# Reordering the tail of a sequence's fourth tile in a two-layer attention and feed-forward kernel (one core)

## The chip, the cores and the metric

The kernel runs on one core of one Trainium2 chip. The metric is the device time of one execution in microseconds, the median of three runs for the kernel before.

## The reference

An input of 8 x 512 x 256 passes a depth-2 transformer, a test-time-training layer, and the same transformer again. Each transformer layer does, with everything in float32:

```python
h = shift_token(x)                       # second half of the channels comes from the row above
q, k, v = jnp.split(h @ wqkv, 3, axis=-1)
q = l2norm(q) * qs;  k = l2norm(k) * ksc
q, k = rotary_xpos(q, k)
o = local_attention(q, k, v)             # windows of 128, each looks at itself and the one before
x = x + o @ wo
h = shift_token(x)
mu = h.mean(-1, keepdims=True);  var = h.var(-1, keepdims=True)
h = (h - mu) / jnp.sqrt(var + 1e-05) * lg + lb
a, g = jnp.split(h @ w1 + b1, 2, axis=-1)
x = x + (a * jax.nn.gelu(g, approximate=False)) @ w2 + b2
```

## The kernel before, in words

There are 4 layers (two before the middle stage, two behind it), and each is run over 8 sequences of 512 rows: 32 sequences in all. A sequence is cut into four tiles of 128 rows, t = 0 to 3. A product is made of three matmuls on split operands (a high and a low part of each side), which stand on lines 1213 to 1215 (`split_product`), so h2T, oT, hT and uT each have a high part, written by ScalarE, and a low part, written by VectorE or GpSimd as the rest.

Each engine has its own instruction list, written out by hand in a function `sequence` of that engine, and semaphores tie the lists together. Every list is worked off strictly in order; a wait holds what stands behind it.

In a tile, TensorE does the scores (`S`, line 1285), the output projection of the tile before (`WO`), q, k and v of the tile ahead (`A1`), transposes of the probabilities (`PT` and `PTE`, lines 1305 and 1312), the value product (`PV`, line 1336) and transposes of the rotated q and k of the tile ahead (`A2`, line 1258). Where it would have to wait, `fill` puts matmuls of the second feed-forward product of the previous sequence (`W2`, line 1471): 16 units for a tile, which the table `cuts` shares out.

Behind the fourth tile comes the feed-forward part. It has two halves of 256 rows each. For each half the normalized rows h2 are made on VectorE (`LN_moments`, `LN_apply`, line 1995) with a power on GpSimd (`LN`, line 708), are transposed on TensorE (`H2T`: line 1375 for the row above the first, line 1377, line 1381), copied out as h2T (ScalarE lines 957 and 959, VectorE lines 1950 and 1951), and multiplied with W1 in six jobs (`W1`): job 0 is the narrow one (6 matmuls), jobs 1 to 5 have 12 each, job 6 to 11 are those of the second half.

Half 0 needs tiles 0 and 1 and the boundary row, so its inputs are there early. Half 1 needs tile 3: behind the last WO, VectorE adds it to Y (`WO`, line 1944), takes the statistics of the half rows (`halves`, lines 1963 and 1964), SyncE's queue moves them by a row with three small transfers (`move_stats`, lines 420, 405 and 423), and then come moments (lines 1979, 1977, 1983), power and apply of the last three columns. TensorE's list has the transposes of half 1 behind job 4 of half 0:

```python
for mt in range(MT):
    W1(L, b, 0, mt, bool(nxt))
    ...
    if mt == 4:
        H2T(L, b, 1)
```

The attention output of the fourth tile is summed in o_sum (`O_first` on ScalarE, `O_add` on VectorE, line 1931), its high part is copied by ScalarE (line 931) and its low part made by VectorE (`O`, line 1937).

Of the kernel before, what the change touches and what calls it, by code (L numbers as in the profile page):

```python
# [39 lines left out]
P = 128  # L40
# [19 lines left out]
E_BANK = 3  # L60
O_BANK = (6, 4)
REST = HID - (MT - 1) * P
# [9 lines left out]
def build(nc, A):  # L72
    ctx = ExitStack()
    with ctx:
# [571 lines left out]
        def _(e):  # L646
# [72 lines left out]

            def sequence(L, b, prev, nxt):  # L720
                for t in range(NT):
# [116 lines left out]
        def _(e):  # L838
# [114 lines left out]
            def H2T(L, b, half):  # L953
# [5 lines left out]
                e.activation(columns(h2T, 0, lo, 2 * P), cut(bank[4][:, :], KT), ACT.Copy).then_inc(h2t_hi, 1)  # L959
# [5 lines left out]
            def G(L, b, half, i):  # L965
# [6 lines left out]
                if mt < MT - 1:  # L972
                    e.activation(gg[:, job % 2, :], bank[job % 4][:, 256:512], ACT.Gelu,  # L973
                                 bias=b1[:, L % 2, 1, mt:mt + 1]).then_inc(gelu_done, 1)
                else:
                    e.activation(gg[0:REST, job % 2, :], bank[job % 4][64:64 + REST, 0:256], ACT.Gelu,
# [17 lines left out]
            def sequence(L, b, prev, nxt):  # L994
                for t in range(NT):
# [20 lines left out]
                    if t == 3:  # L1016
                        O(L, b, t)
# [8 lines left out]
                    if t == 3:  # L1026
                        H2T(L, b, 0)
# [182 lines left out]
        def _(e):  # L1210
# [50 lines left out]
            def S(L, b, t, half, more):  # L1261
# [6 lines left out]
                for j in banks:  # L1268
                    if j == 2 and (t < NT - 1 or more):
                        e.wait_ge(ht_lo, at(ht_lo, n + 2))  # L1270
                    if t == 0:
                        e.wait_ge(u_done, at(u_done, 12 * b + (96 * L + j - 3)))
# [94 lines left out]
            def H2T(L, b, half):  # L1367

                done = 9 * b + (72 * L + 4 * half)
                if half == 0:  # L1370
                    e.wait_ge(pt_sb, at(pt_sb, 3 * idx(L, b, 3) + 3))
                    e.wait_ge(o_added, at(o_added, sums(L, b, 3) + 2))
# [5 lines left out]
                for k in range(KT):  # L1378
                    for i in range(2):
                        e.wait_ge(h2n_done, at(h2n_done, done + half + 2 * k + i + 1))  # L1380
                        mm = e.transpose(bank[4][:, (2 * k + i) * P:(2 * k + i + 1) * P],  # L1381
# [3 lines left out]
            def W1(L, b, half, i, more):  # L1385
# [9 lines left out]
                if job < 4:  # L1395
                    e.wait_ge(nb_done, at(nb_done, 4 * n + 4))
                    if more:
                        if job == 0:
                            e.wait_ge(kt_sb, at(kt_sb, n + 2))
                        if job == 1:  # L1400
                            e.wait_ge(qt_sb, at(qt_sb, q_steps(n + 2)))
                        if job == 2:
                            e.wait_ge(ht_lo, at(ht_lo, n + 3))
                else:
                    e.wait_ge(u_done, at(u_done, 12 * b + (96 * L + job - 3)))
                if job == 6:
                    out = bank[job % 4][:, 0:256]
# [8 lines left out]
                for g in range(0 if job == 6 else 2 if mt < MT - 1 else 1):  # L1416
                    for k in range(KT):
                        mm = split_product(bank[job % 4][:, g * 256:(g + 1) * 256],
# [56 lines left out]
            def sequence(L, b, prev, nxt):  # L1475
                for t in range(NT):
                    ahead = (L, b, t + 1) if t < NT - 1 else nxt and (*nxt, 0)
                    ahead2 = (L, b, t + 2) if t < NT - 2 else nxt and (*nxt, t - 2)
                    cuts = ((5, 6, 11, 13, UNITS), (0, 0, 7, UNITS), (0, 0, 7, UNITS), (0, 0, 7, UNITS))[t]
# [30 lines left out]
                    else:  # L1510
                        PV_first(L, b, t)
                    if ahead and t:
# [59 lines left out]
            def mid_zT(p, i, *ks):  # L1572
                e.wait_ge(t_h[i], at(t_h[i], p + 1))
                for k in ks:
# [4 lines left out]
                    else:  # L1579
                        e.wait_ge(u_done, at(u_done, 12 * (B - 1) + 96 * (DEPTH - 1) + 8 + k + 1))  # L1580
# [262 lines left out]
        def _(e):  # L1843
# [5 lines left out]
            def rotary(L, b, t, i, terms=(0, 1)):  # L1849
# [18 lines left out]
                if t == 1:  # L1868
# [77 lines left out]
            def H2T(L, b, half):  # L1946
# [4 lines left out]
                e.tensor_tensor(columns(h2T, 1, lo, 2 * P), cut(bank[4][:, :], KT), columns(h2T, 0, lo, 2 * P), ALU.subtract).then_inc(h2t_lo, 1)  # L1951
# [50 lines left out]
            def U(L, b, half, i):  # L2002
# [10 lines left out]
                e.scalar_tensor_tensor(ut[0:rows, job % 2, :], bank[job % 4][0:rows, 0:256], b1[0:rows, L % 2, 0, mt:mt + 1],  # L2013
# [89 lines left out]
            def sequence(L, b, prev, nxt):  # L2103
                for t in range(NT):
# [28 lines left out]
                    else:  # L2133
                        for j in range(1, 4):
                            if L == 0 and b == 0 and t == 1 and j == 2:
                                entry_apply(0, 3)
                            R(L, b, t, j)
                            if ahead and j == 2:
                                rotary(*ahead, 0)
                        if ahead:  # L2140
                            rotated(*ahead, 0)
                            squares(idx(*ahead), 0)
                        WO(L, b, t - 1)
                        if t == 3:
                            LN_moments(L, b, 0)
                            halves(L, b, t - 1)
                        if ahead:
# [3 lines left out]
                        if L == 0 and b == 0 and t == 3:  # L2151
                            beta()
                        if t < 3:
# [356 lines left out]
```

## Time and profile before

| | |
|---|---|
| median of 3 runs | 2497.58 us (2497.53 to 2497.6) |
| the profiled execution | 2497.31 us |
| its span | 2495.5 us |
| TensorE busy | 2448.4 us, 98% of the span |
| VectorE, ScalarE, GpSimd busy | 79%, 73%, 63% |
| granted TensorE clock | 0.999 |

The profile is one execution. A row of the timeline gives start, length, engine, line, operation and operands; like instructions behind one another are merged (x8), and in brackets stands how long the engine was idle ahead of it and who released it. Matmuls overlap: a matmul's row is 0.28 us long where the next one starts 0.12 us later. So TensorE's start times tell more than its busy time, and a wait under about 0.17 us shows as no idle time at all.

### The profile page before, as it was taken

Reading aid. Unit: us, or ns where it says so; the run is one execution under the profiler, and the core shown is the slowest. Engines: PE = TensorE matmul, PEld = TensorE weight load, DVE = VectorE, ACT = ScalarE, POOL = GpSimd, SP = SyncE. Lnnn points to the kernel's source line nnn. Section 1 sums busy time; section 2 is a strip of 40 time slices with the busy share of each in tenths; the row PEclk is TensorE's granted clock in tenths of the full one; section 3 lists DMA queues with packets and bytes.
Section 4 is the critical chain, followed back from the end, with each engine's and each line's share of the span. In section 5 each row is a group of like instructions: output and inputs, shape, how many; then the busy total and the mean of one; then the engine's idle time right before and its main releaser. Section 6 shows DMA issues by size and latency. Waiting matters only on the chain. (4 is left out here: it accounts for less than half of the span.)

```text
span 2495.5 us, 80211 instructions
## 1 busy us (share of the span) xinstructions
PE 2448.4 (98%) x29515; PEld 2190.9 (88%) x29515; DVE 1981.1 (79%) x6502; ACT 1809.9 (73%) x5232; POOL 1562.9 (63%) x1798
## 2 busy tenths in 40 slices
PE   8999999999999999999999999999999999999999
PEld 7889989999999889998766898999999988999998
DVE  7888888887877887777656888777777788888886
ACT  6778777777777777776554787777777777777776
POOL 6666667666666666665212676666666667666665
PEclk9999999999999999999999999999999999999999
DMA  3122011013000000005101000000003100000000
GB/s 128 38 88 74 26 58 55 28 37 111 17 4 4 3 3 29 4 15 204 36 19 36 4 3 3 4 4 4 4 4 126 37 3 20 20 20 21 21 21 29
DMA packets 80115, 85.04 MB, mean 34 GB/s; under 512 B 38938, under 2 KB 66030, under 8 KB 78574
## 3 DMA queue, kind: packets, MB, share of 16 engines
q1 hardware_dynamic: 78430, 78.45, 9.7%
q8 instruction: 237, 3.88, 0.6%
q10 hardware_dynamic: 1296, 1.46, 0.2%
q14 instruction: 152, 1.25, 0.2%
HBM read 49.53 MB, written 26.74 MB: 31 GB/s over the span
## 5 line engine op out<-in xcount | busy, mean ns | idle before, releaser
L676 POOL TENSOR_TENSOR pr<-pr,rden 128x384 f32<-128x384 f32 (+1 forms) x480 | 410.1, 871 | 273.0 <-DVE rden L1918 268.1
L888 ACT ACTIVATE pr<-pr,nb 128x192 f32<-128x192 f32 (+1 forms) x1024 | 438.0, 430 | 170.5 <-DVE nb L1909 170.5
L1213 PE MATMUL bank<-h2T,w 128*128 128x256 f32 x1344 | 386.0, 287 | 3.2 <-issue 0.9
L1214 PE MATMUL bank<-h2T,w 128*128 128x256 f32 x1344 | 376.9, 280 | 0.0
L1215 PE MATMUL bank<-h2T,w 128*128 128x256 f32 x1344 | 376.8, 280 | 0.0
L1909 DVE CUSTOM_DVE_ANT_0 pr<-bank,maskb,r 128x192 f32<-128x192 f32 (+1 forms) x1024 | 347.4, 393 | 24.9 <-PE bank L1285 23.3
L718 POOL TENSOR_TENSOR uTl<-t,uTh 128x256 fp32r<-128x256 f32 x288 | 218.0, 762 | 181.0 <-ACT uTh L988 147.9
L1213 PE MATMUL bank<-wqkv,hT 128*128 128x512 f32 x768 | 304.9, 397 | 1.8 <-DVE nb L1909 1.5
L1214 PE MATMUL bank<-wqkv,hT 128*128 128x512 f32 x768 | 302.5, 394 | 0.0
L1215 PE MATMUL bank<-wqkv,hT 128*128 128x512 f32 x768 | 300.1, 391 | 0.0
L2013 DVE SCALAR_TENSOR_TENSOR t<-bank,b,t 128x256 f32<-128x256 f32 (+1 forms) x384 | 184.4, 481 | 109.2 <-POOL uTl L718 47.4
L1213 PEld LDWEIGHTS bank<-h2T,w 128*128 128x128 f32 x1344 | 254.0, 189 | 8.4 <-issue 6.2
L1214 PEld LDWEIGHTS bank<-h2T,w 128*128 128x128 f32 x1344 | 256.5, 191 | 0.0
L1215 PEld LDWEIGHTS bank<-h2T,w 128*128 128x128 f32 x1344 | 252.9, 188 | 0.0
L1471 PE MATMUL bank<-w2h,uTh 128*128 128x256 f32 x768 | 224.8, 294 | 0.0
L671 POOL TENSOR_TENSOR r<-ssg,small 128x8 f32<-128x8 f32 x128 | 214.9, 1679 | 10.7
L708 POOL TENSOR_TENSOR rs<-vare,small 128x4 f32<-128x4 f32 (+2 forms) x96 | 95.3, 993 | 200.0 <-DVE vare L1983 199.8
L660 POOL TENSOR_TENSOR r<-ssg,small 128x8 f32<-128x8 f32 x128 | 213.5, 1668 | 8.0
L1285 PE MATMUL bank<-kT,qT 64*64 64x64 f32 (+2 forms) x6656 | 205.9, 263 | 6.3 <-ACT kT L867 3.1
L973 ACT ACTIVATE t<-bank,b 128x256 f32<-128x256 f32 x320 | 150.8, 471 | 80.7 <-PE bank L1215 77.5
L1285 PEld LDWEIGHTS bank<-kT,qT 64*64 64x64 f32 x6656 | 183.8, 132 | 26.0 <-issue 8.4
L988 ACT ACTIVATE uTh<-t 128x256 fp32r<-128x256 f32 (+1 forms) x352 | 145.3, 413 | 80.9 <-DVE t L2013 78.0
(256 smaller groups left out, 7150.9 us busy)
## 6 DMA issues: line engine op xcount, KB each, us to landing
wqkv<-wqkv_split SPq DMA_DIRECT2D x18, 512.0 KB, 6.4
w<-w_split SPq DMA_DIRECT2D x3, 2816.0 KB, 10.8
Y<-in_x SPq DMA_DIRECT2D x8, 512.0 KB, 7.7
stt<-stt SPq DMA_DIRECT2D x256, 3.0 KB
out<-Y SPq DMA_DIRECT2D x8, 512.0 KB, 3.8
h<-out SPq DMA_DIRECT2D x7, 512.0 KB, 3.9
out<-h SPq DMA_DIRECT2D x7, 512.0 KB, 3.0
stt<-stt SPq DMA_DIRECT2D x192, 0.0 KB
```

What stands on the lines that cost most here:

```text
L660: e.tensor_tensor(r[:, t, 0, :], ssg[:, 0, :], minus_half, ALU.pow).then_inc(rk_done, 1)
L671: e.tensor_tensor(r[:, t, 1, :], ssg[:, 1, :], minus_half, ALU.pow).then_inc(rq_done, 1)
L676: e.tensor_tensor(probs(j, t), probs(j, t), rden[:, 2 * j:2 * j + 2].unsqueeze(2).to_broadcast([P, 2, w]), ALU.mult).then_inc(pn_done, 1 i ...
L718: e.tensor_tensor(uTl[:, half, JOBS[i], :], ut[:, job % 2, :], uTh[:, half, JOBS[i], :], ALU.subtract).then_inc(u_lo, 1)
L888: last = e.activation(probs(j, t)[:, g, :], probs(j, t)[:, g, :], ACT.Exp, bias=nb[:, hd:hd + 1], scale=-1.0, accum_out=den[:, hd:hd + 1])
L1213: e.matmul(out, left[0], right[0], start=first, stop=False)
L1214: e.matmul(out, left[0], right[1], start=False, stop=False)
L1215: return e.matmul(out, left[1], right[0], start=False, stop=last)
L1285: m = e.matmul(out[:, to:to + w, :], qT[rows, 0, p, HB * a:HB * a + HB], kT[rows, p, block:block + w, :], start=True, stop=True, skip_grou ...
L1471: mm = e.matmul(bank[bk][:, 0:D], left, right, start=(unit == 0), stop=(unit == UNITS - 1))
L1909: m = e.tensor_tensor_reduce(probs(j, t)[:, g, :], bank[j][:, g * 256:g * 256 + w], far, r[:, t, 1, place(hd):place(hd) + 1], FAR, ALU.add ...
L2013: e.scalar_tensor_tensor(ut[0:rows, job % 2, :], bank[job % 4][0:rows, 0:256], b1[0:rows, L % 2, 0, mt:mt + 1], gg[0:rows, job % 2, :], AL ...
```

## The change

It reorders the end of the fourth tile (t = 3). On TensorE the transposes of half 0's h2 move from behind the last W2 units to directly behind the value product, and job 0 of W1 moves ahead of the fourth tile's WO. Two W2 units move from behind A2 to ahead of the value product (`cuts`: 9 in place of 7). On VectorE the moments of half 0 move up between two reciprocals, the apply moves ahead of the last step of q's rotation, and a few small steps trade places; the low part of the attention output moves from VectorE to GpSimd (`O_lower`). On GpSimd the power moves ahead of the guard and power of k. On ScalarE the copy of h2T's first half moves ahead of the copy of the attention output. Half 0's transposes go to bank 3, and the W1 jobs take banks 2, 1, 0, 3 in place of 0, 1, 2, 3.

```diff
+H2T_BANK = (3, 4)
+JOB_BANK = (2, 1, 0, 3)
...
+            def O_lower(L, b, t):
+
+                n = idx(L, b, t)
+                for i in pair:
+                    e.wait_ge(o_hi, at(o_hi, 2 * n + i + 1))
+                    e.tensor_tensor(oT[:, 1, 2 * i:2 * i + 2, :].rearrange("p a c -> p (a c)"), o_sum[:, 2 * P * i:2 * P * i + 2 * P],
+                                    oT[:, 0, 2 * i:2 * i + 2, :].rearrange("p a c -> p (a c)"), ALU.subtract).then_inc(o_lo, 1)
...
+                    if t == 3:
+                        LN(L, b, 0)
                     if ahead and t:
                         guard_k(*ahead)
                     if ahead:
                         A1_k(*ahead)
                     if t == 3:
-                        LN(L, b, 0)
+                        O_lower(L, b, t)
...
                     if t == 3:
+                        H2T(L, b, 0)
                         O(L, b, t)
...
-                    if t == 3:
-                        H2T(L, b, 0)
...
-                    e.wait_ge(o_added, at(o_added, sums(L, b, 3) + 2))
...
-                    cuts = ((5, 6, 11, 13, UNITS), (0, 0, 7, UNITS), (0, 0, 7, UNITS), (0, 0, 7, UNITS))[t]
+                    cuts = ((5, 6, 11, 13, UNITS), (0, 0, 7, UNITS), (0, 0, 7, UNITS), (0, 0, 9, UNITS))[t]
...
+                    if t == 3:
+                        H2T(L, b, 0)
+                        fill(2)
...
-                    if t:
+                    if t in (1, 2):
                         fill(2)
-                    if t == 3:
-                        H2T(L, b, 0)
-                        WO(L, b, t)
                 for mt in range(MT):
                     W1(L, b, 0, mt, bool(nxt))
+                    if mt == 0:
+                        WO(L, b, 3)
...
+                            if t == 3 and j == 1:
+                                LN_moments(L, b, 0)
...
+                            LN_apply(L, b, 0)
+                            if ahead:
+                                rotated(*ahead, 1)
...
-                        LN_apply(L, b, 0)
-                        O(L, b, t)
+                        H2T(L, b, 0)
                         if prev:
                             W2(*prev, t)
-                        H2T(L, b, 0)
+                        if ahead:
+                            squares(idx(*ahead), 1)
```

Three places show it. TensorE behind the value product (pT, v) of the fourth tile, second sequence of the first layer. Before, the eight transposes of q and k follow, then W2 units:

```order
L1336 MATMUL bank<-pT,v 64x128 x16
L1336 MATMUL bank<-pT,v 64x64 x16
L1258 MATMUL bank<-ident,t 128x128 x8
L1471 MATMUL bank<-w2l,uTh 128x256
L1471 MATMUL bank<-w2h,uTl 128x256
```

Now (in the changed kernel's line numbers) the h2 transposes come first and then the W2 units:

```order
L1347 MATMUL bank<-pT,v 64x128 x16
L1347 MATMUL bank<-pT,v 64x64 x16
L1385 MATMUL bank<-lead,pick 128x2
L1391 MATMUL bank<-ident,h 128x128 x4
L1481 MATMUL bank<-w2h,uTh 128x256
L1481 MATMUL bank<-w2l,uTh 128x256
```

So the h2 transposes no longer stand behind the q and k transposes and nine W2 units. A little later on TensorE, before, all twelve matmuls of WO (wo, oT) stand ahead of W1 (h2T, w):

```order
L1213 MATMUL bank<-wo,oT 128x256
L1214 MATMUL bank<-wo,oT 128x256
L1215 MATMUL bank<-wo,oT 128x256
L1213 MATMUL bank<-h2T,w 128x256
L1214 MATMUL bank<-h2T,w 128x256
L1215 MATMUL bank<-h2T,w 128x256
```

Now six matmuls of W1's job 0 follow the q and k transposes, and WO begins behind them:

```order
L1269 MATMUL bank<-ident,t 128x128 x8
L1224 MATMUL bank<-h2T,w 128x256
L1225 MATMUL bank<-h2T,w 128x256
L1226 MATMUL bank<-h2T,w 128x256
L1224 MATMUL bank<-h2T,w 128x256
L1225 MATMUL bank<-h2T,w 128x256
L1226 MATMUL bank<-h2T,w 128x256
L1224 MATMUL bank<-wo,oT 128x256
L1225 MATMUL bank<-wo,oT 128x256
```

WO has six matmuls of W1 ahead of it that stood behind it. VectorE in the same tile, before, from the sums of q's squares to h2T's low part (h is h2, t are the rotation's buffers):

```order
L1896 TENSOR_REDUCE ssq<-sq 128x8
L1871 TENSOR_TENSOR t<-bank,rot 128x512
L1875 TENSOR_TENSOR t<-bank,rot 128x512
L1882 TENSOR_TENSOR t<-t 128x512
L1847 TENSOR_TENSOR hT<-bank,hT 128x2x128
L1931 TENSOR_TENSOR qT<-bank,qT 128x256 x2
L1991 TENSOR_TENSOR lead<-mv,rs 128x2
L1995 TENSOR_SCALAR h<-Y,mv,rs 128x128 x4
L1937 TENSOR_TENSOR oT<-qT,oT 128x256 x2
L2029 TENSOR_TENSOR Y<-bank,xb 128x256
L1950 TENSOR_TENSOR h2T<-bank,h2T 128x1
L1951 TENSOR_TENSOR h2T<-bank,h2T 128x2x256
```

Now:

```order
L1908 TENSOR_REDUCE ssk<-sq 128x8
L1883 TENSOR_TENSOR t<-bank,rot 128x512
L1887 TENSOR_TENSOR t<-bank,rot 128x512
L2003 TENSOR_TENSOR lead<-mv,rs 128x2
L2007 TENSOR_SCALAR h<-Y,mv,rs 128x128 x4
L1894 TENSOR_TENSOR t<-t 128x512
L1859 TENSOR_TENSOR hT<-bank,hT 128x2x128
L1943 TENSOR_TENSOR qT<-bank,qT 128x256 x2
L1962 TENSOR_TENSOR h2T<-bank,h2T 128x1
L1963 TENSOR_TENSOR h2T<-bank,h2T 128x2x256
L2041 TENSOR_TENSOR Y<-bank,xb 128x256
L1908 TENSOR_REDUCE ssq<-sq 128x8
```

The four h2 instructions stand three places earlier, the low part of oT is gone from this list, and the sum of q's squares stands at its end.

## Rows read from the trace of the kernel before

**Rows 1.** The page: busy time and share of each engine.

```profile
PE 2448.4 (98%) x29515; PEld 2190.9 (88%) x29515; DVE 1981.1 (79%) x6502; ACT 1809.9 (73%) x5232; POOL 1562.9 (63%) x1798
```

**Rows 2.** Waits of TensorE: total us, times, longest.

```profile
PE bank L1258 <- DVE t L1882: 9.4, 26, 0.4
```

**Rows 3.** Timeline of TensorE, fourth tile of one sequence: start, length.

```profile
1831.07 1.57 PE L1336 MATMUL bank<-pT,v 64*64 64x128 f32 x64
1833.00 1.09 PE L1258 MATMUL bank<-ident,t 128*128 128x128 f32 x8 [0.36 <-DVE t L1882]
1833.85 0.36 PE L1471 MATMUL bank<-w2l,uTh 128*128 128x256 f32 x1
...
1834.98 0.28 PE L1375 MATMUL bank<-lead,pick 128*128 128x2 f32 x2
...
1835.57 0.35 PE L1213 MATMUL bank<-wo,oT 128*128 128x256 f32 x1
...
1836.94 0.28 PE L1215 MATMUL bank<-wo,oT 128*128 128x256 f32 x1
1837.35 0.36 PE L1213 MATMUL bank<-h2T,w 128*128 128x256 f32 x1
1837.55 0.28 PE L1214 MATMUL bank<-h2T,w 128*128 128x256 f32 x1
```

**Rows 4.** Timeline of TensorE, third tile of the same sequence.

```profile
1817.77 1.57 PE L1336 MATMUL bank<-pT,v 64*64 64x128 f32 x64
1819.27 1.09 PE L1258 MATMUL bank<-ident,t 128*128 128x128 f32 x8
```

**Rows 5.** Timelines of VectorE and SyncE's queue behind the fourth tile's WO.

```profile
1837.33 0.43 DVE L1944 TENSOR_TENSOR Y<-bank,Y 128x256 f32<-128x256 f32 x1
1841.74 0.21 DVE L1979 BATCH_NORM_AGGREGATE mv<-stt 128x2 f32<-128x12 f32 x1 [1.60 <-DMA stt<-stt]
1843.32 0.86 DVE L1995 TENSOR_SCALAR h<-Y,mv,rs 128x128 f32<-128x128 f32 x3 [0.15 <-issue]
...
1839.89 0.82 SPq L423 DMA_DIRECT2D stt<-stt  x1
```

**Rows 6.** Timelines of TensorE, then VectorE: half 1's h2 in the last sequence.

```profile
2474.75 0.94 PE L1381 MATMUL bank<-ident,h 128*128 128x128 f32 x4
...
2474.45 0.86 DVE L1995 TENSOR_SCALAR h<-Y,mv,rs 128x128 f32<-128x128 f32 x3 [0.15 <-issue]
```

**Rows 7.** Timeline of TensorE: half 1's transposes in the sequence of rows 3.

```profile
1843.90 0.66 PE L1381 MATMUL bank<-ident,h 128*128 128x128 f32 x4
```

**Rows 8.** Timelines of TensorE, then VectorE: half 1's h2 in the fifth sequence.

```profile
373.63 0.60 PE L1381 MATMUL bank<-ident,h 128*128 128x128 f32 x4
...
372.14 0.86 DVE L1995 TENSOR_SCALAR h<-Y,mv,rs 128x128 f32<-128x128 f32 x3 [0.15 <-issue]
```

**Rows 9.** Timelines of ScalarE and VectorE: o_sum's first copies, h2T's low part.

```profile
1832.77 0.66 ACT L917 ACTIVATE qT<-bank 128x256 f32<-128x256 f32 x2 [0.54 <-PE bank L1336]
...
1836.56 0.68 DVE L1951 TENSOR_TENSOR h2T<-bank,h2T 128x512 fp32r<-128x512 f32 x1
```

**Rows 10.** Timelines of VectorE, then GpSimd, fourth tile: hole, moments, rotation, h2, power.

```profile
1826.36 0.17 DVE L1918 RECIPROCAL rden<-den 128x2 f32<-128x2 f32 x1 [0.64 <-ACT pr L888]
...
1829.38 0.27 DVE L1979 BATCH_NORM_AGGREGATE mv<-stt 128x2 f32<-128x12 f32 x2
...
1829.83 0.17 DVE L1983 TENSOR_SCALAR vare<-mv 128x4 f32<-128x4 f32 x1
...
1832.20 0.75 DVE L1882 TENSOR_TENSOR t<-t 128x512 f32<-128x512 f32 x1
...
1833.98 1.12 DVE L1995 TENSOR_SCALAR h<-Y,mv,rs 128x128 f32<-128x128 f32 x4
...
1832.36 1.46 POOL L708 TENSOR_TENSOR rs<-vare,small 128x4 f32<-128x4 f32 x1
```

**Rows 11.** GpSimd's line 718 over the whole kernel: min/median/max ns.

```profile
L718 POOL TENSOR_TENSOR uTl<-t,uTh x288: 724/740/1365, 88.8 to 2485.9; 128x256 fp32r<-128x256 f32 x144
```

More of the change, by code:

```diff
@@ L958, in H2T @@
                 lo = half * 2 * P
-                e.activation(columns(h2T, 0, lo, 2 * P), cut(bank[4][:, :], KT), ACT.Copy).then_inc(h2t_hi, 1)
+                e.activation(columns(h2T, 0, lo, 2 * P), cut(bank[H2T_BANK[half]][:, :], KT), ACT.Copy).then_inc(h2t_hi, 1)
             def table(func):
@@ L1380, in H2T @@
                         e.wait_ge(h2n_done, at(h2n_done, done + half + 2 * k + i + 1))
-                        mm = e.transpose(bank[4][:, (2 * k + i) * P:(2 * k + i + 1) * P],
+                        mm = e.transpose(bank[H2T_BANK[half]][:, (2 * k + i) * P:(2 * k + i + 1) * P],
                                          h2[:, 2 * half + i, k * P:(k + 1) * P], ident[:, :])
@@ L1406, in W1 @@
                 if job == 6:
-                    out = bank[job % 4][:, 0:256]
+                    out = bank[JOB_BANK[job % 4]][:, 0:256]
                     for k in range(KT):
@@ L1417, in W1 @@
                     for k in range(KT):
-                        mm = split_product(bank[job % 4][:, g * 256:(g + 1) * 256],
+                        mm = split_product(bank[JOB_BANK[job % 4]][:, g * 256:(g + 1) * 256],
                                            [w1[:, k, s_, g * HP + mt * P:g * HP + (mt + 1) * P] for s_ in range(HL)],
@@ L1867, in rotary @@
                 e.wait_ge((kt_ps, qt_ps)[i], at((kt_ps, qt_ps)[i], (m, q_steps(m))[i]))
-                if t == 1:
+                if t == 1 or t == 0 and i == 1:
                     e.wait_ge((sqk, sqq)[i], at((sqk, sqq)[i], m + 1))
@@ L1950, in H2T @@
                 e.tensor_tensor(h2T[:, 1, c:c + 1], bank[5][:, src:src + 1], h2T[:, 0, c:c + 1], ALU.subtract)
-                e.tensor_tensor(columns(h2T, 1, lo, 2 * P), cut(bank[4][:, :], KT), columns(h2T, 0, lo, 2 * P), ALU.subtract).then_inc(h2t_lo, 1)
+                e.tensor_tensor(columns(h2T, 1, lo, 2 * P), cut(bank[H2T_BANK[half]][:, :], KT), columns(h2T, 0, lo, 2 * P), ALU.subtract).then_inc(h2t_lo, 1)
             def no_neighbour():
@@ L2012, in U @@
                 rows = P if mt < MT - 1 else REST
-                e.scalar_tensor_tensor(ut[0:rows, job % 2, :], bank[job % 4][0:rows, 0:256], b1[0:rows, L % 2, 0, mt:mt + 1],
+                e.scalar_tensor_tensor(ut[0:rows, job % 2, :], bank[JOB_BANK[job % 4]][0:rows, 0:256], b1[0:rows, L % 2, 0, mt:mt + 1],
                                        gg[0:rows, job % 2, :], ALU.add, ALU.mult).then_inc(u_done, 1)
@@ L2137, in sequence @@
                             R(L, b, t, j)
+                            if t == 3 and j == 1:
+                                LN_moments(L, b, 0)
                             if ahead and j == 2:
                                 rotary(*ahead, 0)
-                        if ahead:
+                        if t == 3:
+                            if ahead:
+                                rotated(*ahead, 0)
+                            WO(L, b, t - 1)
+                            halves(L, b, t - 1)
+                            if ahead:
+                                squares(idx(*ahead), 0)
+                                rotary(*ahead, 1)
+                            LN_apply(L, b, 0)
+                            if ahead:
+                                rotated(*ahead, 1)
+                            if L == 0 and b == 0:
+                                beta()
+                        else:
                             rotated(*ahead, 0)
                             squares(idx(*ahead), 0)
[L2143 to L2147, printed above, removed]
+                            WO(L, b, t - 1)
                             squares(idx(*ahead), 1)
@@ L2169, in sequence @@
                     if t == 3:
[L2170 to L2171 removed]
+                        H2T(L, b, 0)
                         if prev:
                             W2(*prev, t)
[L2174 removed]
+                        if ahead:
+                            squares(idx(*ahead), 1)
                         tile2_told(L, b)
```

15 lines of the change are left out of this document (6 added, 9 removed).

## The prediction, on record before the changed kernel ran

> **What bounds the kernel now.** I began with the page. TensorE is busy 98% of the span [rows 1], so a change can only win what TensorE still waits, or lose by making it wait. Then I read who it waits for: the largest entry is 9.4 us in 26 waits for VectorE's last step of the rotation, at the q transposes [rows 2]. This is a list of idle time, and matmuls overlap, so I read start times in the timeline of one sequence of the third layer, which stands for most of the others.
>
> In its fourth tile the value product starts at 1831.07 and the q transposes at 1833.00, 1.93 later [rows 3]. In the third tile the same two are 1.50 apart with no wait [rows 4]. So 0.43 us is lost there. The second loss is at W1: WO's last matmul starts at 1836.94 and W1's first at 1837.35 [rows 3]. Matmuls of this form follow each other by 0.117 us (WO's twelve take 1.37 from first to last start, of which the first takes 0.20 behind a transpose), so 0.29 us is lost. W1 waits for h2T's low part, which ends at 1836.56 + 0.68 = 1837.24 [rows 9]. The change aims at these two, 0.72 us of a sequence, or 23 us over 32 sequences.
>
> The question is what else ties TensorE down behind them. Half 1's transposes stand behind W1's job 4 and need the rows of tile 3, which start from WO's end. That chain is serial: add to Y at 1837.33, statistics, three transfers issued one by one, the last at 1839.89 + 0.82, an idle VectorE that waits 1.60 us for their landing until 1841.74, then moments, power, and the three last h2 instructions from 1843.32 to 1844.18 [rows 5]. From WO's last start, 1836.94, it is 7.24 us. In the same sequence the four transposes start at 1843.90 and their row ends at 1844.56 [rows 7], 0.38 us behind the last h2.
>
> Is that 0.38 a chance or a tie? In the last sequence the row of the four is stretched to 0.94 us and ends at 2475.69, again 0.38 behind the last h2, which ends at 2475.31 [rows 6]. There TensorE clearly waits. In the fifth sequence, where TensorE's list has extra matmuls in between, the row is 0.60 long and ends at 374.23, 1.23 behind the h2 that ends at 373.00 [rows 8]; there the h2 was early. So 0.38 is the least distance. I read these two ends in all 32 sequences: 27 have 0.38 or 0.39, two 0.46 and 0.52, and three (the fifth to seventh) 1.0 to 1.23, a slack of up to 0.85 [rows 8]. In the steady sequence the row is 0.66, only 0.06 over the free one: TensorE arrives just as the h2 does. The fourth tile's WO therefore starts a chain that has no slack, and whoever delays WO's end delays TensorE 7.24 us later.
>
> **The change, part by part,** on the clock of rows 3.
>
> Two more W2 units ahead of the value product: 2 x 0.117 = 0.23. It starts at 1831.30 and ends its turn 1.50 later [rows 4], at 1832.80.
>
> The h2 transposes follow at once, if h2 is there. VectorE's new order: the moments need 0.62 us (1829.38 to 1829.83 + 0.17) and fit the 0.64 us in which it idles ahead of the third reciprocal at 1826.36 [rows 10]. They cost nothing; if they were 0.2 late, the rotation, and nothing on TensorE at once, would be. Ahead of the apply two sums and two moments less, one add and the statistics as before: the two rotation products end at about 1831.1 in place of 1832.1, so h2's four instructions (1.12 us [rows 10]) end at about 1832.3, 0.5 before TensorE comes. They also need the power on GpSimd, 1.46 us here [rows 10]; ahead of the guard it starts when the last normalization ends, at 1829.2, and is done by 1830.7. No wait.
>
> The transposes take 1834.98 to 1835.57, 0.59 [rows 3]: to 1833.39. Seven W2 units take 0.20 + 6 x 0.117 = 0.90: to 1834.29. The rotated q is then done at about 1833.0 and the 0.43 wait is gone; k's multiply on GpSimd, later by the power, ends near 1834.1, ahead of its transposes at 1834.7. Both sets of transposes take 1833.00 to 1833.85, 0.85 [rows 3]: to 1835.14.
>
> W1's job 0 needs h2T. From the first h2 transpose to W1's first start it was 1837.35 - 1834.98 = 2.37 with both copies at once behind the transposes [rows 3]. From 1832.80 that is 1835.17, so its wait is nearly gone (0.03). ScalarE's o_sum copies, 0.66 us long and started 1.70 behind the value product's start [rows 9], end at 1833.66, as the transposes' results come out. Job 0 is six matmuls, 0.20 + 5 x 0.117 = 0.79: to 1835.96.
>
> WO, twelve matmuls with no change of form ahead, takes 12 x 0.117 = 1.40: to 1837.36, its last start at 1837.25. Its low operand now comes from GpSimd: two instructions, each like line 718's, median 0.74 us [rows 11], from ScalarE's high part at about 1834.7: ready at 1835.45 and 1836.2, needed at 1835.96 and 1836.67. They are hidden with 0.5 to spare.
>
> So job 1 of W1 starts at 1837.36; before, it would be 1837.35 + 0.79 = 1838.14. Up to here 0.78 us is won. But WO's last start moved from 1836.94 to 1837.25, by **+0.31**: job 0's 0.79 stands ahead of it, against 0.43 of wait and a 0.09 change of form won (the rest is rounding of the slots). The last h2 follows by 7.24: 1844.49 in place of 1844.18. TensorE comes to the four transposes four jobs behind 1837.36, at 1843.1, and would be through them by about 1843.5; it waits about 1.1 us. Everything behind moves with h2: the 0.78 is given back and 0.31 more is paid. The rest of the sequence has no wait that could take this up.
>
> Sum: 29 sequences x 0.31 = +9.0. In the three with slack, 0.85 of it turns into 0.54 won each [rows 8]: -1.6. Together +7.4 us. The profiled execution took 2497.31, so 2504.7; the median of the runs is 0.27 above it, so **2505.0 us**.
>
> The bounds of 0.31: below, 0.15, if the chain behind WO gets some 0.15 shorter (VectorE waits 1.60 for the transfers in it, so a lighter VectorE list gives little). Above, 0.6, if h2T's copies or the low part on GpSimd come 0.3 late. That makes +3 to +16, 2500 to 2514.
>
> A rule that speaks against the move to GpSimd: VectorE made both low parts in the time that one costs GpSimd, and line 718's slowest took 1365 ns against a median of 740 [rows 11]; which partner on VectorE stretches it, this row does not tell. The Trainium skill ("SBUF — State Buffer", Who interferes with whom) says that a VectorE instruction with two SBUF inputs blocks GpSimd's reads. By it the two new instructions would run beside h2T's low part, a sum and the W2 add, none of which reads SBUF twice, and stay at 0.74; blocked twice they would be 1.37 each, which is the second rival.
>
> **The rivals.**
> - *Half 1 is not tied to WO* (faster). If the 0.38 were only where TensorE's list happens to end, 0.78 us would stay won in about 28 sequences: -22 us, 2476. For it: in the steady row the stretch is only 0.06. Against it: the last sequence is stretched by 0.34 and ends at the same 0.38. It decides at about 0.15 us of hidden slack. 0.12.
> - *The low part or h2T comes late* (slower still). At 1.37 each, GpSimd's second part is ready at 1837.4 in place of 1836.67, so WO ends 0.8 later: (0.31 + 0.8) x 32 = +35, 2532. Half a contention, or 0.2 us more in h2T's copies, is +6: 2511. For it: ScalarE's list is tight there. Against it: 0.5 of room. 0.13.
> - *Gain and loss cancel* (no change). If the chain shortens by 0.2 or the slack sequences win more, the shift is 0.1 or less: 2500 to 2502. 0.14.
> - The forecast, a shift of 0.2 to 0.45: 2502 to 2509. 0.61.
>
> **How the numbers follow.** A difference of 0.2% (5 us) is about what a measurement of this kernel can tell from none. The forecast lies wholly above it but for its lowest end, 0.05. Slower: 0.56 + 0.13 = 0.69; same: 0.14 + 0.05 = 0.19; faster: 0.12. The range 2500 to 2512 holds the forecast, the cancelling case and the small half of the late one.
>
> **What the new profile would show.** The wait of rows 2 shrinks to 1 us or less. A new one stands first: the second group of h2 transposes (now line 1391) waits for VectorE's h2 in some 28 sequences, 0.9 to 1.0 us each by the idle column, while TensorE's busy time hardly changes. W1's first start comes 3.9 us behind the value product's, not 6.3. WO's last start is 5.95 behind the value product's start, against 5.87; the last h2 stays 7.2 behind it. If that last distance shrinks, or if the new wait is not there, the forecast is wrong. If WO's operands show idle time ahead of it, the second rival is right.

## The result, and the profile after

Over six runs each on the same chips the changed kernel took 2514.22 us (2513.18 to 2515.46), the kernel before 2496.82: a ratio of 1.0068, 95% interval 1.0057 to 1.008. The forecast was 2505.0 within 2500 to 2512. The direction was right, the loss more than twice what was forecast, and the time lies outside the range. The profiled execution took 2515.46 with a span of 2513.7, so 18.2 more than the one of before.

Busy time on the page of the changed kernel [rows 1 for before]:

```profile
PE 2459.1 (98%) x29515; PEld 2192.6 (87%) x29515; DVE 1966.7 (78%) x6438; ACT 1809.1 (72%) x5232; POOL 1607.7 (64%) x1862
```

GpSimd has 64 instructions more, 32 times the two of `O_lower`. Two waits of TensorE in the changed kernel, the largest and one that the text comes back to, total us, times, longest [rows 2 for before]:

```profile
PE bank L1391 <- DVE h L2007: 19.4, 30, 1.5
...
PE bank L1316 <- POOL pr L678: 2.7, 5, 1.3
```

The wait for the rotation is gone, and one for h2 has taken its place, in the step and at the line that were forecast. The wait for GpSimd's normalization was there before too, at the same place (line 1305 there), with 1.6 us in 4 times. TensorE's timeline of the changed kernel in the fourth tile of the same sequence [rows 3 for before]:

```profile
1840.79 1.24 PE L1316 MATMUL bank<-ident,pr 128*128 128x128 f32 x8
...
1843.67 1.57 PE L1347 MATMUL bank<-pT,v 64*64 64x128 f32 x64
1845.17 0.38 PE L1385 MATMUL bank<-lead,pick 128*128 128x2 f32 x2
1845.41 0.64 PE L1391 MATMUL bank<-ident,h 128*128 128x128 f32 x4
1845.80 0.37 PE L1481 MATMUL bank<-w2h,uTh 128*128 128x256 f32 x1
...
1846.72 1.04 PE L1269 MATMUL bank<-ident,t 128*128 128x128 f32 x8
1847.64 0.36 PE L1224 MATMUL bank<-h2T,w 128*128 128x256 f32 x1
...
1848.42 0.28 PE L1224 MATMUL bank<-wo,oT 128*128 128x256 f32 x1
...
1849.72 0.28 PE L1226 MATMUL bank<-wo,oT 128*128 128x256 f32 x1
...
1856.50 0.84 PE L1391 MATMUL bank<-ident,h 128*128 128x128 f32 x3 [0.60 <-DVE h L2007]
1857.10 0.37 PE L1224 MATMUL bank<-h2T,w 128*128 128x256 f32 x1
```

WO's last matmul starts 6.05 us behind the value product's start (1849.72 - 1843.67), where 5.95 was forecast and 5.87 stood before. VectorE's three last h2 instructions of half 1, in the same kernel:

```profile
1856.10 0.86 DVE L2007 TENSOR_SCALAR h<-Y,mv,rs 128x128 f32<-128x128 f32 x3 [0.15 <-issue]
```

They end at 1856.96, 7.24 behind WO's last start, exactly as before. TensorE arrives at half 1's transposes at about 1855.5 and waits.

The starts of WO's last matmul in all 32 sequences, set against those of before, give the period, the time from one sequence to the next: in the steady sequences it grew from about 70.18 to 70.82, by 0.61 to 0.64 us each. WO's new place explains only part of it. WO's last matmul starts 0.18 later behind the value product's start (6.05 against 5.87), and two more W2 units, 0.23, stand ahead of the value product: 0.41 to 0.42 together. Some 0.21 must arise ahead of the value product, and there the first row above already differs. The eight transposes of the probabilities wait for GpSimd's normalization, and this for VectorE's reciprocals. In the kernel before, two of the reciprocals (the second and the fourth), GpSimd's first three normalizations and the eight transposes were:

```profile
1825.57 0.15 DVE L1918 RECIPROCAL rden<-den 128x2 f32<-128x2 f32 x1
...
1827.65 0.15 DVE L1918 RECIPROCAL rden<-den 128x2 f32<-128x2 f32 x1
...
1825.06 2.40 POOL L676 TENSOR_TENSOR pr<-pr,rden 128x384 f32<-128x384 f32 x3 [2.80 <-DVE rden L1918]
...
1828.62 1.04 PE L1305 MATMUL bank<-ident,pr 128*128 128x128 f32 x8
```

VectorE in the changed kernel [rows 10 for before]:

```profile
1837.73 0.16 DVE L1930 RECIPROCAL rden<-den 128x2 f32<-128x2 f32 x1
1837.81 0.25 DVE L1991 BATCH_NORM_AGGREGATE mv<-stt 128x2 f32<-128x12 f32 x2
1837.99 0.22 DVE L1989 BATCH_NORM_AGGREGATE mv<-stt 128x2 f32<-128x12 f32 x2
1838.25 0.62 DVE L1995 TENSOR_SCALAR vare<-mv 128x4 f32<-128x4 f32 x1
1838.78 0.15 DVE L1930 RECIPROCAL rden<-den 128x2 f32<-128x2 f32 x1
...
1840.04 0.15 DVE L1930 RECIPROCAL rden<-den 128x2 f32<-128x2 f32 x1
```

And GpSimd's normalizations beside them:

```profile
1837.23 1.61 POOL L678 TENSOR_TENSOR pr<-pr,rden 128x384 f32<-128x384 f32 x2 [2.80 <-DVE rden L1930]
1839.01 0.83 POOL L678 TENSOR_TENSOR pr<-pr,rden 128x384 f32<-128x384 f32 x1 [0.17 <-DVE rden L1930]
1840.27 1.26 POOL L678 TENSOR_TENSOR pr<-pr,rden 128x384 f32<-128x384 f32 x1 [0.43 <-DVE rden L1930]
```

The instruction that adds epsilon to four variances takes 0.62 us in its new place, against 0.17 in the old one [rows 10]. It ends at 1838.87, just when GpSimd's second normalization does (1837.23 + 1.61 = 1838.84). The third reciprocal comes 1.05 us behind the second, against 0.79 before (1825.57 to 1826.36), the fourth 2.31 behind it against 2.08. GpSimd, which had its third normalization right behind the second, now idles 0.17.

In one sequence the early moments cost more. They wait for the transfers of the third tile's statistics, and in the sixteenth sequence, the last ahead of the middle stage, these land late: the issue of the second one takes 5.50 us, 1.8 behind a load of rot (in the kernel before 4.37, in the sequence of rows 3 0.83). VectorE idles 1.50 us, the third reciprocal comes 2.19 behind the second (1139.97 - 1137.78), and TensorE waits:

```profile
1132.03 5.50 SPq L407 DMA_DIRECT2D stt<-stt  x1
...
1139.43 0.28 DVE L1991 BATCH_NORM_AGGREGATE mv<-stt 128x2 f32<-128x12 f32 x2 [1.50 <-DMA stt<-stt]
...
1139.97 0.27 DVE L1930 RECIPROCAL rden<-den 128x2 f32<-128x2 f32 x2
...
1141.10 0.44 PE L1316 MATMUL bank<-ident,pr 128*128 128x128 f32 x2 [1.28 <-POOL pr L678]
```

In the kernel before, the moments stand behind the fourth reciprocal, and TensorE's longest wait in this sequence's transposes is 0.35.

So two theories stood for the experiments: (1) WO behind job 0 costs 0.4 a sequence through the chain of 7.24, and (2) the early moments cost 0.2 through the reciprocals. The rival to (1) is that TensorE's own order costs the time, the rival to (2) that the 0.2 belongs to something else, the banks or GpSimd's longer list.

### The profile page after: what moved, and what is told of

Read it like the earlier page. It is cut to its first block and busy times, and to the rows that moved or that the text cites. A ratio compares the mean times of both kernels' runs of the same rounds, so it can differ in the third digit from the quotient of the medians.

```text
span 2513.7 us, 80211 instructions
## 1 busy us (share of the span) xinstructions
PE 2459.1 (98%) x29515; PEld 2192.6 (87%) x29515; DVE 1966.7 (78%) x6438; ACT 1809.1 (72%) x5232; POOL 1607.7 (64%) x1862
## 5 line engine op out<-in xcount | busy, mean ns | idle before, releaser
L673 POOL TENSOR_TENSOR r<-ssg,small 128x8 f32<-128x8 f32 x128 | 213.4, 1667 | 10.7
L900 ACT ACTIVATION_READ_ACCUMULATOR pr<-pr,nb 128x1 f32 x1024 | 191.7, 187 | 0.0
```

The source lines that it names most:

```text
L673: e.tensor_tensor(r[:, t, 1, :], ssg[:, 1, :], minus_half, ALU.pow).then_inc(rq_done, 1)
L900: last = e.activation(probs(j, t)[:, g, :], probs(j, t)[:, g, :], ACT.Exp, bias=nb[:, hd:hd + 1], scale=-1.0, accum_out=den[:, hd:hd + 1])
```

## The experiments

Periods and distances below are read from start times on TensorE in each kernel's timeline, as above. "pick" is the start of the first matmul of h2's transposes of half 0.

### WO ahead of W1 again

```diff
+                WO(L, b, 3)
                 for mt in range(MT):
                     W1(L, b, 0, mt, bool(nxt))
-                    if mt == 0:
-                        WO(L, b, 3)
```

> The changed kernel, with the fourth tile's WO ahead of job 0 of W1 again and nothing else undone. Theory A (the last h2 of a sequence follows WO's last start by 7.24 us, whatever stands between, and TensorE waits for it): WO moves up by at most 0.79 us, but its low operand comes from GpSimd at about 2.7 and 3.4 us behind the first h2 transpose, so its last start moves from 4.55 to about 4.1, and 0.45 us is won in each of some 29 sequences: -13 us against the changed kernel. Rival B (the loss has nothing to do with WO's end): the new wait for the low operand is only added, +0.3 us a sequence, +10 us.

Measured: 2504.15 us (2503.47 to 2505.28), ratio to the kernel before 1.0029 (1.0018 to 1.0041). 10.1 of the 17.4 went with this one edit, 3 less than expected. Its largest wait on TensorE, and the place in the timeline:

```profile
PE bank L1224 <- POOL oT L727: 11.4, 32, 1.1
```

```profile
1840.07 1.04 PE L1269 MATMUL bank<-ident,t 128*128 128x128 f32 x8
1841.35 0.35 PE L1224 MATMUL bank<-wo,oT 128*128 128x256 f32 x1 [0.25 <-POOL oT L727]
```

WO now waits for the low part on GpSimd and starts 2.84 behind pick; without that wait it would be about 2.47. The period is about 70.43, some 0.4 below the changed kernel's. The last h2 stays 7.24 behind WO's last start in the steady sequences.

### Moments back behind the rotated k

```diff
-                            if t == 3 and j == 1:
-                                LN_moments(L, b, 0)
...
                             if ahead:
                                 rotated(*ahead, 0)
+                            LN_moments(L, b, 0)
                             WO(L, b, t - 1)
```

> The changed kernel, with the moments of half 0 moved back on VectorE, behind the fourth reciprocal and the rotated k; they still stand ahead of WO's add. Theory A (moved up they make the third and fourth reciprocal 0.23 to 0.26 us late, because the last moment instruction takes 0.62 us in place of 0.17 beside GpSimd, and with them the fourth normalization and the probability transposes): the 0.2 us ahead of the value product is gone in 31 sequences, -6 us. Rival B (the late reciprocal is covered, the 0.2 us has another cause, such as the other banks): no change, within 1 us.

Measured: 2506.54 us (2506.42 to 2507.83), ratio 1.004 (1.0027 to 1.0052), so 7.7 less than the changed kernel. The wait at line 1316 is 1.3 us in 3 times, no more than in the kernel before, and the sixteenth sequence has none of 1.28; the wait at line 1391 stays (19.1 us in 30), and the period is 70.56 to 70.61. The instruction that adds epsilon now starts in the last part of GpSimd's fourth normalization. It takes 0.34 and again ends with it, at 1834.55 against 1833.26 + 1.26 = 1834.52:

```profile
1834.21 0.34 DVE L1995 TENSOR_SCALAR vare<-mv 128x4 f32<-128x4 f32 x1
...
1833.26 1.26 POOL L678 TENSOR_TENSOR pr<-pr,rden 128x384 f32<-128x384 f32 x1 [0.42 <-DVE rden L1930]
```

The h2 of half 0 comes later (its last instruction ends 0.1 behind pick, not 0.6 ahead of it), and nobody waits for it.

### The early moments alone, in the kernel before

The same edit the other way round, with everything else as before: the call of `LN_moments(L, b, 0)` moves from behind the rotated k to between the second and the third reciprocal.

> The kernel before, with one part of the change alone: the moments of half 0 between the second and third reciprocal. Theory A (the late reciprocal): +0.2 us in some 31 sequences, +6 us against the kernel before, and a wait for GpSimd's normalization at the last probability transposes. Rival B: within 1 us of the kernel before.

Measured: 2504.15 us (2501.85 to 2505.43), ratio 1.0029 (1.0016 to 1.0041): this one move costs the kernel before 7.1 us by the medians, and 4.9 by the spans of the two profiled executions (2500.4 and 2495.5), with a steady period 0.2 us longer. Its rows on VectorE show the same stretch, with no new bank and no `O_lower` in the program:

```profile
1828.39 0.62 DVE L1983 TENSOR_SCALAR vare<-mv 128x4 f32<-128x4 f32 x1
1828.93 0.15 DVE L1918 RECIPROCAL rden<-den 128x2 f32<-128x2 f32 x1
```

TensorE's wait for the normalization is 2.4 us in 7 times, where the kernel before had 1.6 in 4:

```profile
PE bank L1305 <- POOL pr L676: 2.4, 7, 0.5
```

### Only the epsilon instruction back

In the changed kernel the four aggregates stay between the reciprocals; the one TENSOR_SCALAR goes behind the fourth reciprocal.

```diff
                 m.then_inc(mv_done, 1)
-                e.wait_ge(mv_done, at(mv_done, 3 * b + (24 * L + part + 1)))
+                if part:
+                    LN_eps(L, b, part)
+
+            def LN_eps(L, b, part):
+                half, lo, hi = LN_PARTS[part]
+                e.wait_ge(mv_done, at(mv_done, 3 * b + (24 * L + part + 1)))
...
+                            LN_eps(L, b, 0)
                             if ahead:
                                 rotated(*ahead, 0)
```

> The changed kernel, with the four moment instructions left in the hole ahead of the third reciprocal and only the last one, which adds epsilon to the variance (128 x 4), moved behind the fourth reciprocal. Theory A (that one instruction is stretched from 0.17 to 0.62 us beside GpSimd's normalization and makes the reciprocals late): the third reciprocal is on time, and as in the experiment that moves all of them, -6 to -8 us against the changed kernel. Rival B (it is the four aggregates, or their number, that make it late): the changed kernel's time within 2 us.

Measured: 2508.06 us (2506.17 to 2511.1), ratio 1.0047 (1.0034 to 1.006): 6.2 less than the changed kernel, so about 6 of the 7 to 8 us of the moments hang on this one instruction. The aggregates still wait for the transfers in the sixteenth sequence, where VectorE idles 0.94. VectorE in this kernel:

```profile
1832.43 0.22 DVE L1989 BATCH_NORM_AGGREGATE mv<-stt 128x2 f32<-128x12 f32 x2
1832.98 0.17 DVE L1930 RECIPROCAL rden<-den 128x2 f32<-128x2 f32 x1 [0.33 <-ACT pr L900]
...
1834.26 0.15 DVE L1930 RECIPROCAL rden<-den 128x2 f32<-128x2 f32 x1
1834.33 0.15 DVE L2000 TENSOR_SCALAR vare<-mv 128x4 f32<-128x4 f32 x1
```

The aggregates fit the idle time with 0.33 left, and the instruction takes 0.15 while GpSimd is idle. Its neighbour begins at 1834.50:

```profile
1831.67 2.40 POOL L678 TENSOR_TENSOR pr<-pr,rden 128x384 f32<-128x384 f32 x3 [2.81 <-DVE rden L1930]
1834.50 1.27 POOL L678 TENSOR_TENSOR pr<-pr,rden 128x384 f32<-128x384 f32 x1 [0.43 <-DVE rden L1930]
```

The Trainium skill ("SBUF — State Buffer", Who interferes with whom) says that a VectorE `tensor_scalar` can enter a mode that takes the port pair which it shares with GpSimd, and that whoever issues second then blocks until the other's instruction is through. The rows beside a normalization agree: 0.62 us in one place and 0.34 in another, each ending with it, and 0.15 with GpSimd idle. One row does not: in the kernel before, the same instruction starts 0.28 behind GpSimd's power and takes 0.17, though the power runs 1.2 us longer. So blocking through the whole of the other's instruction holds here beside the normalization and not beside the power. That the mode was entered is inferred; no run here changed the instruction's form in its place.

### More work for TensorE behind W1's job 3

```diff
+                    if mt == 3:
+                        busy(6, 5)
```

In the changed kernel, six transposes that nobody needs stand in front of job 4, some 0.66 us of TensorE.

> The changed kernel with six transposes of the identity matrix (0.66 us and a change of form, together about 0.75) between job 3 and job 4 of W1 in half 0, where they write a bank that nothing reads. It does more work and computes the same. Theory A (TensorE waits 1.1 to 1.5 us for h2 behind job 4 whatever it does before): within 2 us of the changed kernel. Rival B (TensorE's own work sets the pace): +0.75 x 32 = +24 us.

Measured: 2514.29 us (2513.67 to 2518.21), against 2514.22. TensorE comes to half 1's transposes 11.01 behind pick instead of 10.34, and the last of them still starts 11.84 behind it; the four behind the first are stretched to 1.05 us, where 0.60 is the free length [rows 8]:

```profile
1854.80 1.05 PE L1391 MATMUL bank<-ident,h 128*128 128x128 f32 x4
```

0.66 us of added work in each of 32 sequences costs nothing, so TensorE's own length does not set the period there. The first experiment, in which an earlier WO shortened the period, shows that the chain behind WO does.

### Both undone

> The changed kernel with both undone: WO ahead of job 0, the moments behind the fourth reciprocal. If the two causes add (theory A): 2514.2 - 10.1 - 7.7 = 2496.5, the time of the kernel before within 2 us; TensorE still waits about 0.4 us a sequence for GpSimd's low part. Rival B (they share a cause, so that one hides behind the other): above 2500.

The edits of the first two experiments together. Measured: 2497.46 us (2495.57 to 2500.97, 11 runs), ratio 1.0005 (0.9996 to 1.0014): no difference from the kernel before. The two edits taken singly gave 10.1 and 7.7, both at once 16.8: they add up within about 1 us, and they are the whole loss. What is left of the change is early h2 transposes, nine W2 units ahead of the value product, the low part on GpSimd, the banks, and the smaller moves on VectorE, GpSimd and ScalarE. TensorE waits for GpSimd's low part 11.3 us in 32 times, and the period is 70.22 to 70.30.

### The low part on VectorE as well

```diff
-                    if t == 3:
-                        O_lower(L, b, t)
...
                     if t == 3:
+                        O(L, b, t)
                         H2T(L, b, 0)
```

GpSimd's `O_lower` goes; `O` on ScalarE and on VectorE stands ahead of `H2T`, since W1 no longer needs h2T first.

> As the one with both undone, and the low part of the attention output on VectorE again, ahead of h2T's low part, with ScalarE's high part ahead of its h2T copy. Theory A: WO's last start comes 3.8 us behind the first h2 transpose in place of 4.2, the last h2 7.24 behind that; 0.4 us x 30 less, 2486 us. Rival B (GpSimd's low part was hidden): no change against the one with both undone.

Measured: 2487.49 us (2485.04 to 2489.42), ratio 0.9963 (0.9951 to 0.9976). This version beats both kernels: 9 us under the kernel before. WO starts 2.48 behind pick and its last matmul 3.85, where the changed kernel had 4.55. TensorE in this kernel:

```profile
1825.92 0.38 PE L1383 MATMUL bank<-lead,pick 128*128 128x2 f32 x2
...
1827.47 1.04 PE L1267 MATMUL bank<-ident,t 128*128 128x128 f32 x8
1828.40 0.35 PE L1222 MATMUL bank<-wo,oT 128*128 128x256 f32 x1
...
1836.38 1.12 PE L1389 MATMUL bank<-ident,h 128*128 128x128 f32 x4
```

The last row is stretched, so half 1's transposes still wait for h2 (by about 0.5 us, 1.12 against 0.60); the tie has not gone, its start has moved forward. The chain behind it has grown: the last h2 comes 7.34 behind WO's last start. VectorE's add of WO stands behind the sum of q's squares and begins at 1830.28, 0.51 behind WO's last start instead of 0.39. ScalarE's order changed too, but its high part starts 1.45 behind pick here and 1.47 in the version before, so the gain is VectorE's: its two low parts end 2.33 and 2.67 behind pick, GpSimd's ended 2.70 and 3.38.

### Five W2 units behind WO

`cuts` for t = 3 becomes (0, 0, 7, 11, UNITS): seven units ahead of the value product, none between the h2 transposes and A2, four behind A2, five behind WO; VectorE's addition of W2 moves behind half 1's moments.

> As the one with the low part on VectorE, and the W2 units shared out so that four stand ahead of WO and five behind it (seven ahead of the value product, as before), with VectorE's W2 add behind the statistics of tile 3. Theory A: WO's last start 3.3 us behind the first h2 transpose, the last h2 at 10.6, and TensorE comes to its last transpose only at 10.8: no wait is left, 0.8 us a sequence won against the kernel before, 2472 us. Rival B (something else ties half 1's transposes, or the copies of q and k come late for the next tile): 2480 us or more.

A miss: 2495.09 us (2493.73 to 2496.41), ratio 0.9993 (0.9984 to 1.0002), where the theory gave 2472. The tie was loosened (the last transpose starts 0.29 after h2 is done), but the transposes of the rotated k came too early:

```profile
1832.47 0.66 PE L1267 MATMUL bank<-ident,t 128*128 128x128 f32 x4
1833.37 0.66 PE L1267 MATMUL bank<-ident,t 128*128 128x128 f32 x4 [0.25 <-POOL t L665]
```

The q and k sets are 0.90 apart instead of about 0.45, and the four transposes of q start 0.97 behind pick, some 0.3 later than their place allows. WO starts 2.83 behind pick. The period is 70.11, where the version with the low part on VectorE has 70.03, so the tie's wait has gone and nothing was won by it.

These rows are not the whole of the 7.6 us that lie between this version and that one. By WO's starts the profiled executions differ by 6.1: 1.8 in the three slack sequences and 3.6 at one place, behind the ninth sequence. There SyncE's load of weights (raw_w), which stands ahead of WO's last start in the other versions, stands 0.90 behind it, and the issue of the second transfer takes 3.31 us instead of 0.83:

```profile
650.55 0.39 SPq L463 DMA_DIRECT2D raw_w<-in_w  x1
...
651.70 3.31 SPq L407 DMA_DIRECT2D stt<-stt  x1
```

The chain behind WO is 9.69 there. That the load lengthens the issue is read from where it stands; no run moved it alone.

### Two W2 units behind WO

`cuts` (0, 0, 7, 14, UNITS), with seven units between the h2 transposes and A2 as in the version with the low part on VectorE.

> The kernel e7_low_on_vector with two of the nine W2 units ahead of the fourth tile's value product moved behind WO, and VectorE's addition of the W2 result moved behind half 1's moments to match; seven units still stand between the h2 transposes and the q and k transposes, so the rotated q and k are there in time (in e8_w2_behind_wo they were not). The value product, the h2 transposes and WO can start 0.23 us earlier, the transposes of half 1 still arrive at their place 0.4 us ahead of the last h2. Theory A (TensorE waits 0.4 us a sequence at half 1's transposes, because WO starts too late): the period falls from 70.05 by 0.15 to 0.25 in some 28 sequences, to 2480 to 2484. Rival B: h2 of half 0, or VectorE's low part of the attention output, does not come any earlier, so TensorE stands 0.1 to 0.2 at its transposes or at WO, WO's start moves by under 0.1 against the sequence, and the time stays at 2485 to 2489.

Measured: 2487.21 us (2484.3 to 2489.07), ratio 0.996 (0.9947 to 0.9974), no different from 2487.49; the rival held for the time. Its steady period is 69.84 to 69.92, 0.15 less than there, but the medians do not show it; part of it was eaten in the ninth sequence, as in the experiment before. The load stands behind WO's last start again, the issue of the second transfer takes 2.92, the chain behind WO 9.31, and the period across it is 73.26. These two versions, both with the later W2 units and the later addition, are the only ones of the eleven traces in which this happens. WO starts 2.7 behind pick, not 2.48, which is no gain, since pick itself has moved forward by the two units' 0.23. What shortens the period is the chain behind WO: it is 7.24 again, because VectorE, rid of the W2 addition ahead of it, adds WO 0.39 behind its last start and not 0.51. VectorE's low part and WO in this kernel:

```profile
1828.20 0.76 DVE L1948 TENSOR_TENSOR oT<-qT,oT 128x256 fp32r<-128x256 f32 x2 [0.21 <-ACT oT L941]
```

```profile
1828.77 0.36 PE L1222 MATMUL bank<-wo,oT 128*128 128x256 f32 x1
```

WO starts 0.57 behind the low part's start, here as in the version with all units ahead (there 1827.83, 1828.40), and in both the low part starts 2.92 behind the first h2 instruction, with VectorE busy between but for 0.2. In that version TensorE's own list led to the same time: the eight transposes ahead of WO start at 1827.47 and take 0.92. Here they start at 1827.62, so WO could start at 1828.54 and starts 0.23 later. So the list of VectorE ahead of the low part now sets WO's start. That this is the next bound is read from two traces; no run removed it.

## Why the prediction was right in direction and wrong in size

**The bound and the tie: right.** The 7.24 us between WO's last start and the last h2 stood in the steady sequences of the changed kernel and of the first experiment, to 0.01 or 0.02. The added transposes show that TensorE has slack ahead of it. The first rival (no tie, 2476) is refuted.

**The wait that disappears and the one that appears: right.** Line 1258's wait (9.4) is gone, line 1391 waits in 30 places. By the idle column it is 0.65 on average where 0.9 to 1.0 was forecast. Matmuls overlap, so the column is short by a part of each: the five transposes and the step to W1 take 0.46 in the slack sequences of the kernel before, so W1 would follow at 1855.97 and follows at 1857.10, that is 1.1, as forecast. TensorE's busy time was to stay as it was and grew by 10.7 us (2448.4 to 2459.1), since a row that waits half-way is stretched and counts as busy.

**The shift of WO: mechanism right, term too small.** 0.31 was forecast behind the value product. Three small terms of its sum were low: the h2 transposes took 0.63 (1845.17 to 1845.80) where rows 3 gave 0.59: the first of them follows the pick matmuls by 0.24, not 0.14 (1834.98 to 1835.12 before), when these stand directly behind the value product; seven W2 units took 0.92, not 0.90; the q and k transposes took 0.92 (1846.72 to 1847.64), not 0.85. Together 0.13, of which a forecast remainder of 0.03 is taken up: W1 starts 2.47 behind pick, not 2.37. Its operand, h2T's low part, ends at 1847.54, so both ways lead to that time. The shift is thus 0.41 to 0.42, and undoing it gave about 0.4 a sequence, 10.1 us in all, even though GpSimd's low part then cost WO about 0.37 itself. Expected were 13.

**The early moments: the step that failed.** "They cost nothing; if they were 0.2 late, the rotation, and nothing on TensorE at once, would be." Both halves were wrong. The duration of the epsilon instruction, 0.17, was taken from a place where GpSimd works on other things, to a place beside a normalization, where it takes 0.62. And behind it stood not only the rotation but the third and fourth reciprocal, on which GpSimd's normalization, the transposes of the probabilities, the value product and everything after it depend. 0.23 at the fourth reciprocal arrived as 0.21 in the period: 7.7 us by undoing it, 7.1 by doing it alone, 6.2 by the one instruction. The prediction also left out that the moments wait for the transfers, which held back the third reciprocal of the sixteenth sequence and gave TensorE its wait of 1.28 us. The fault could be seen: the idle time was 0.64 long, the moments 0.62, and a fit of 0.02 bears no stretch at all; the prediction weighed the port rule against the two new instructions on GpSimd and not against the one moved on VectorE.

**GpSimd's low part: right where it stood.** The two instructions took 0.74 each, 1.43 together, the lower of the prediction's two prices, and were done at 1848.56, ahead of the second half of WO at 1849.13. The second rival (2511 to 2532) named the right amount of harm by a wrong cause. But with WO ahead of W1 the same two instructions are the longest wait, 11.4 us, and the version with the low part back on VectorE is 10.0 us faster (2497.46 to 2487.49).

**The slack sequences: right in mechanism.** The fifth to seventh had 1.0 to 1.2 us at the tie's place and have 0.38 now. From WO's starts they gained 2.6 us against the steady pace, the forecast's 0.85 each. Set against a loss of 0.63 and not of 0.31, that leaves 0.7 us won in the three, not the forecast's 1.6.

**The sum.** 29 x 0.42 = 12.2, 29 x 0.21 = 6.1, less 0.7: 17.6, against 17.4 in the medians. That it closes to 0.2 is in part luck, since the steady pace does not hold everywhere. By WO's starts the profiled execution, the slowest of the six, is 18.0 longer from the first sequence to the last. Of this, 25 periods share 14.8, 0.59 each; the three slack ones are -0.7; and the three about the middle stage make 3.9 where 1.9 would be their share. The wait of 1.28 in the sixteenth sequence is in these three and cannot account for them alone: in the kernel with the extra transposes, which has a wait of 1.50 there, they lost 1.9, and the period across the middle stage alone lies between 272.0 and 274.7 us in the eleven traces, in no order that fits an edit. What moves it was not tried.

## What to carry to other kernels

When an instruction is moved into an idle gap, compare what runs beside it in the new place with what ran beside it in the old one, and look at what is queued behind the gap: a gap of 0.64 us filled with 0.62 us has no margin, and if the next instruction feeds the critical path the whole stretch arrives there. Where a chain without slack begins at a point (here WO's end), order the work by that point: here removing a wait of 0.4 us elsewhere was worth nothing, and 0.4 us ahead of that point was paid in full. A mixed change is best taken apart edit by edit: here one edit cost 10 us, one 7.7, and a third (the low part on GpSimd) showed its price only when these were undone; what remained made the kernel 9 us faster than before.

## What the runs showed of the hardware that was not expected

- A VectorE TENSOR_SCALAR of 128x4 elements that began while GpSimd's normalization of 128x384 ran took 0.62 us in the changed kernel and in the kernel before with early moments, and 0.34 with the moments back, where it began nearer to the normalization's end. In all three it ended 0.02 to 0.03 us behind the normalization. With GpSimd idle it took 0.15, and beside GpSimd's power of 128x8 in the kernel before 0.17 [rows 10]:

```profile
1829.55 1.67 POOL L660 TENSOR_TENSOR r<-ssg,small 128x8 f32<-128x8 f32 x1
```

- The first step from one form of matmul to another on TensorE was not of one length: the first h2 transpose follows the two pick matmuls by 0.24 us when they stand directly behind the 64-wide value product, and by 0.14 behind W2's matmuls [rows 3 for the pick]. What makes the difference was not tried.
- The issue of the second of the statistics transfers on SyncE's queue took 0.83 us as a rule. In every trace it took 4.1 to 5.5 at three places, each 1.8 us behind a load of rot, and in two traces 2.92 and 3.31, 1.51 and 1.16 us behind a load of raw_w. What lengthens it was not tried.
